# Mixture-of-experts tail: expert tiles of 128 slots in pairs, and second weights held in SBUF

## The reference, cut to what matters

```
logits = einsum('btd,ed->bte', x, w_router); probs = softmax(logits)
vals, idx = top_k(probs, 2); gates = sum(one_hot(idx, 8) * vals[..., None], -2)
acc = gelu(x @ Ws1.T + bs1) @ Ws2.T + bs2              # shared expert, 128 -> 512 -> 128
h = gelu(einsum('btd,efd->btef', x, W1) + b1)           # 8 experts, 128 -> 512 -> 128
y = einsum('btef,edf->bted', h, W2) + b2
out = SCALE * (acc + einsum('bted,bte->btd', y, gates))
```

## Time and profile before

| | |
|---|---|
| median of 3 runs (lowest to highest) | 633.46 us (633.27 to 637.78) |
| profiled execution | 635.85 us |
| its span, first to last instruction | 634.1 us |
| mean granted TensorE clock | 0.976 |
| TensorE matmul busy over the span | 576.8 us, 91% |

### The profile page before, as it was taken

The page is one execution under the profiler, slowest core; times in us unless marked ns, Lnnn a source line. Parts: engine busy times, 40 slices in busy tenths (PEclk is TensorE's granted clock), DMA queues, the critical chain, the costliest instruction groups (busy, mean ns, idle before and its releaser), DMA issues. The chain is left out here.

```text
span 634.1 us, 14457 instructions
## 1 busy us (share of the span) xinstructions
PE 576.8 (91%) x4324; PEld 512.9 (81%) x4324; DVE 427.3 (67%) x1730; ACT 333.7 (53%) x1064; POOL 389.8 (61%) x598
## 2 busy tenths in 40 slices
PE   2469999999999999999996967899999999999976
PEld 2249999899999999999984566788999999999952
DVE  3736888788788888878885579876553455545426
ACT  2455666566666656666662374894444444444410
POOL 1526666656666665666662607888888888887520
PEclk9999999999999999999998869899999999999989
DMA  9069930000000000000000001163564778777357
GB/s 196 6 260 394 395 150 1 2 0 0 0 0 0 0 0 0 0 0 0 2 2 1 2 0 39 45 231 95 156 186 130 216 244 247 230 235 232 103 201 212
DMA packets 39797, 66.77 MB, mean 105 GB/s; under 512 B 7523, under 2 KB 26725, under 8 KB 39749
## 3 DMA queue, kind: packets, MB, share of 16 engines
q1 hardware_dynamic: 31076, 54.85, 27.5%
q0 software_dynamic: 4544, 9.45, 4.2%
q10 hardware_dynamic: 4128, 1.91, 1.4%
HBM read 36.26 MB, written 29.92 MB: 104 GB/s over the span
## 5 line engine op out<-in xcount | busy, mean ns | idle before, releaser
L1575 ACT ACTIVATE hid<-bank,slab 128x256 f32<-128x256 f32 x156 | 64.2, 471 | 80.6 <-PE bank L1428 80.5
L1987 POOL DMA_INDIRECT ys<-yo,dst x78 | 75.2, 964 | 28.9 <-issue 16.6
L1979 POOL DMA_INDIRECT xs<-hrow,slot_i x64 | 62.7, 979 | 35.4 <-issue 35.4
L1442 PEld LDWEIGHTS bank<-slab,hid 128*128 128x128 f32 x624 | 75.8, 192 | 2.0
L1442 PE MATMUL bank<-slab,hid 128*128 128x128 f32 x624 | 76.0, 275 | 0.0
L1428 PE MATMUL bank<-hg,slab 128*128 128x256 f32 x312 | 73.7, 380 | 0.4 <-DVE hg L1842 0.4
L1875 DVE TENSOR_TENSOR yb<-bank,slab 128x256 f32<-128x256 f32 x39 | 16.6, 425 | 74.1 <-PE bank L1442 74.1
L1428 PEld LDWEIGHTS bank<-hg,slab 128*128 128x128 f32 x312 | 56.3, 190 | 6.7 <-issue 0.6
L986 POOL TENSOR_TENSOR nL<-aL,ones 128x128 f32<-128x128 bf16 x32 | 16.9, 528 | 41.4 <-ACT aL L695 41.4
L409 PE MATMUL bank<-aH,W2p 128*128 128x128 f32 x192 | 42.1, 301 | 0.1
L409 PE MATMUL bank<-kv,W1b 128*128 128x128 f32 x192 | 41.4, 298 | 0.0
(11 more groups left out here) (340 smaller groups left out, 1872.3 us busy)
## 6 DMA issues: line engine op xcount, KB each, us to landing
slab<-in_slabs_dram SPq DMA_DIRECT2D x39, 578.0 KB, 4.2
xs<-fill SPq DMA_DIRECT2D x34, 528.0 KB
xt<-xs SPq DMA_DIRECT2D x39, 132.0 KB
yg<-ys SPq DMA_DIRECT2D x8, 512.0 KB, 6.7
xr<-in_L_attn_x_dram SPq DMA_DIRECT2D x16, 128.0 KB, 6.9
ys<-yo,dst POOLq DMA_INDIRECT x78, 3.8
xs<-hrow,slot_i POOLq DMA_INDIRECT x64, 2.5
out_dram<-xr SPq DMA_DIRECT2D x16, 64.0 KB, 1.8
```

The lines of the kernel that those rows point to most:

```text
L1442: mm = pe.matmul(y[:, s * D:(s + 1) * D], hid[i % 2][:, n, s * P:(s + 1) * P], right, start=(n == 0), stop=(n == FT - 1), skip_group_check ...
L1575: nc.scalar.activation(hid[i % 2][:, n, :], e_half(i, n), ACT.Gelu_apprx_tanh, bias=bias).then_inc(e_x, 1)
L1979: pool.indirect_dma_start(out=xs[:, :], out_offset=bass.IndirectOffsetOnAxis(ap=slot_i[:, i, c:c + 1], axis=0), in_=hrow[:, c, :], in_offs ...
L1987: pool.indirect_dma_start(out=ys[:, :], out_offset=bass.IndirectOffsetOnAxis(ap=dst[v][:, s:s + 1], axis=0), in_=yo[v][:, s, :], in_offset ...
```

## The change

Tiles are allotted in halves of 128 slots, and a job is two halves that may belong to two different experts. 8192/128 + 7 = 71 halves, rounded up to 72, make 36 jobs in place of 39. `N_FULL` becomes 12. The list has 43 jobs; five shared ones still come before the second part of the expert jobs, now in front of expert job 12. The second weights of all 8 experts (2 MB) are loaded into SBUF once, at the start of the block, and TensorE addresses them by a register that it loads itself, two loads a job. The slab shrinks from 1156 to 644 numbers and is loaded twice a job, as are the rows, each half with its own register load on SP. `RW` goes from 5 to 4. The first matmul is done by halves: eight matmuls of 128 columns in place of four of 256; the gelu also, eight instructions in place of four.

```diff
-SLAB = 2 * F + FT + D
-N_TILES = (2 * B * S) // TS + E - 1
+SLAB = F + FT + D
+HALF = P
+N_HALVES = -(-((2 * B * S) // HALF + E - 1) // SUB) * SUB
+N_TILES = N_HALVES // SUB
-N_FULL = -(-(B * S - E * (TS - 1)) // TS)
+N_FULL = -(-(B * S - E * (HALF - 1)) // HALF) // SUB
+FULL = N_FULL * SUB
-RW = 5
+RW = 4
...
+            w2 = psb("w2", [P, E, F])
-            hid = [psb(f"hid{i}", [P, FT, TS]) for i in range(2)]
+            hid = hs
...
                 def weights(j):
                     if j >= RW:
                         sp.wait_ge(e_yb, job["expert", j - RW] + 1)
-                    e = sp.value_load(e_i[0:1, j:j + 1], min_val=0, max_val=E - 1)
-                    sp.dma_start(slab[j % RW][:, :], slabs[:, bass.ds(e, 1), :].rearrange("p o w -> p (o w)")).then_inc(s_slab[j % RW], 16)
+                    for s in range(SUB):
+                        e = sp.value_load(e_i[0:1, SUB * j + s:SUB * j + s + 1], min_val=0, max_val=E - 1)
+                        sp.dma_start(slab[j % RW][:, s, :], slabs[:, bass.ds(e, 1), :].rearrange("p o w -> p (o w)")).then_inc(s_slab[j % RW], 16)
                 def rows(j):
...
-                    row = sp.value_load(row_i[0:1, j:j + 1], min_val=0, max_val=XS_ROWS - TS)
-                    sp.dma_start(xt[j % RX][:, :, :], xs[bass.ds(row, TS), :].rearrange("(s p) w -> p s w", p=P)).then_inc(s_xt[j % RX], 16)
-
+                    for s in range(SUB):
+                        row = sp.value_load(row_i[0:1, SUB * j + s:SUB * j + s + 1], min_val=0, max_val=XS_ROWS - HALF)
+                        sp.dma_start(xt[j % RX][:, s, :], xs[bass.ds(row, HALF), :]).then_inc(s_xt[j % RX], 16)
+
+                sp.dma_start(w2[:, :, :], e_w2).then_inc(s_w2, 16)
                 sp.wait_ge(table_ready, 2)
...
                     for n in range(FT):
-                        mm = pe.matmul(e_half(i, n), left[:, n * P:(n + 1) * P], right, start=True, stop=True)
+                        if kind == "expert":
+                            for s in range(SUB):
+                                mm = pe.matmul(e_half(i, n)[:, s * P:(s + 1) * P], slab[j % RW][:, s, n * P:(n + 1) * P],
+                                               hg[j % 2][:, s * P:(s + 1) * P], start=True, stop=True)
+                        else:
+                            mm = pe.matmul(e_half(i, n), left[:, n * P:(n + 1) * P], right, start=True, stop=True)
...
                 def e_down(i):
+                    if kind == "expert":
+                        if j == 0:
+                            pe.wait_ge(s_w2, 16)
+                            pe.wait_ge(table_ready, 2)
+                        if j == N_FULL:
+                            pe.wait_ge(table_ready, 4)
+                        expert = [pe.value_load(e_i[0:1, SUB * j + s:SUB * j + s + 1], min_val=0, max_val=E - 1) for s in range(SUB)]
...
-                            right = slab[j % RW][:, F + n * P:F + (n + 1) * P] if kind == "expert" else sw[:, 1, n, :]
+                            right = w2[:, bass.ds(expert[s], 1), n * P:(n + 1) * P].rearrange("p o w -> p (o w)") if kind == "expert" else sw[:, 1, n, :]
...
-                        nc.scalar.activation(hid[i % 2][:, n, :], e_half(i, n), ACT.Gelu_apprx_tanh, bias=bias).then_inc(e_x, 1)
+                        if kind == "expert":
+                            nc.scalar.activation(hid[i % 2][:, n, 0:P], e_half(i, n)[:, 0:P], ACT.Gelu_apprx_tanh,
+                                                 bias=slab[j % RW][:, 0, F + n:F + n + 1])
+                            nc.scalar.activation(hid[i % 2][:, n, P:TS], e_half(i, n)[:, P:TS], ACT.Gelu_apprx_tanh,
+                                                 bias=slab[j % RW][:, 1, F + n:F + n + 1]).then_inc(e_x, 1)
```

More of the change, by code:

```diff
@@ L128, in program @@
         at = 0
-        for name, width in (("iota", E), ("down", E), ("tri", E * E), ("step", CAP // TS), ("tile", N_TILES), ("tau", CH), ("dump", SUB * RY), ("b2row", D)):
+        for name, width in (("iota", E), ("down", E), ("tri", E * E), ("step", CAP // HALF), ("tile", N_HALVES), ("tau", CH), ("dump", SUB * RY), ("b2row", D)):
             cut[name] = tabs[:, at:at + width]
@@ L1210, in program @@
             base, cnt, need, last = (psb(n, [P, E]) for n in ("base", "cnt", "need", "last"))
-            over = psb("over", [P, E, CAP // TS])
+            over = psb("over", [P, E, CAP // HALF])
             tri = psb("tri", [P, E, E])
-            past = psb("past", [P, N_TILES, E])
+            past = psb("past", [P, N_HALVES, E])
             full, taken, weight = psb("full", [P, E]), psb("taken", [P, E + 1]), psb("weight", [P, E])
-            first, rowf = psb("first", [P, N_TILES]), psb("rowf", [P, N_TILES])
+            first, rowf = psb("first", [P, N_HALVES]), psb("rowf", [P, N_HALVES])
             hs = [psb(f"hs{i}", [P, FT, SH]) for i in range(2)]
@@ L1218, in program @@
             xt = [psb(f"xt{i}", [P, SUB, ROW]) for i in range(RX)]
-            slab = [psb(f"slab{i}", [P, SLAB]) for i in range(RW)]
+            slab = [psb(f"slab{i}", [P, SUB, SLAB]) for i in range(RW)]
+            w2 = psb("w2", [P, E, F])
             hg = [psb(f"hg{i}", [P, TS]) for i in range(2)]
-            hid = [psb(f"hid{i}", [P, FT, TS]) for i in range(2)]
+            hid = hs
             yb = [psb(f"yb{i}", [P, SUB, D]) for i in range(2)]
@@ L1244, in program @@
             s_yg = [sem(f"s_yg{i}") for i in range(NG)]
-            s_slab = [sem(f"s_slab{i}") for i in range(RW)]
+            s_slab, s_w2 = [sem(f"s_slab{i}") for i in range(RW)], sem("s_w2")
             meta_step, meta_ready = sem("meta_step"), sem("meta_ready")
@@ L1573, in e_gelu @@
                         act.wait_ge(e_u, 2 * i + n // 2 + 1)
-                        bias = slab[j % RW][:, 2 * F + n:2 * F + n + 1] if kind == "expert" else sb1[:, n:n + 1]
-                        nc.scalar.activation(hid[i % 2][:, n, :], e_half(i, n), ACT.Gelu_apprx_tanh, bias=bias).then_inc(e_x, 1)
+                        if kind == "expert":
[3 more added lines that the diff above has]
+                                                 bias=slab[j % RW][:, 1, F + n:F + n + 1]).then_inc(e_x, 1)
+                        else:
+                            nc.scalar.activation(hid[i % 2][:, n, :], e_half(i, n), ACT.Gelu_apprx_tanh, bias=sb1[:, n:n + 1]).then_inc(e_x, 1)
                 def to_exp():
@@ L1784, in steps_over @@
                                                   op0=ALU.mult, op1=ALU.add))
-                    then(dve.scalar_tensor_tensor(out=over[:, :, :], in0=cnt[:, :].unsqueeze(2).broadcast_to([P, E, CAP // TS]),
-                                                  scalar=-float(spare), in1=cut["step"].unsqueeze(1).broadcast_to([P, E, CAP // TS]),
+                    then(dve.scalar_tensor_tensor(out=over[:, :, :], in0=cnt[:, :].unsqueeze(2).broadcast_to([P, E, CAP // HALF]),
+                                                  scalar=-float(spare), in1=cut["step"].unsqueeze(1).broadcast_to([P, E, CAP // HALF]),
                                                   op0=ALU.add, op1=ALU.is_gt))
@@ L1821, in full_tiles @@
                     row_of(ts, full, 0)
-                    then(dve.tensor_scalar(last[:, :], last[:, :], float(N_FULL), None, ALU.min))
+                    then(dve.tensor_scalar(last[:, :], last[:, :], float(FULL), None, ALU.min))
                     then(dve.memset(taken[:, E:E + 1], 0.0))
@@ L1827, in other_tiles @@
                 def other_tiles():
-                    ts = slice(N_FULL, N_TILES)
+                    ts = slice(FULL, N_HALVES)
                     steps_over(0)
```

46 lines of the change are left out of this document (22 added, 24 removed).

## The result

| | before | after |
|---|---|---|
| median of the runs beside each other | 635.62 us (633.27 to 640.31, 4 runs) | 652.57 us (646.65 to 654.83, 4 runs) |
| ratio, 95% interval | | 1.0226 (1.0163 to 1.0289) |
| profiled execution, span | 635.85, 634.1 us | 651.17, 649.4 us |

The change makes the kernel slower. The forecast was 642.5, with slower at 0.69: the sign and the range hold, the median lies 10 us above the number. Later runs of the same changed kernel gave 650.09 (ratio 1.0224, 1.0163 to 1.0285).

The account below looks back on a forecast made before the run. TensorE's matmuls were taken to bound the kernel before, SP's issues afterwards: TensorE's 9.4 us gain turns into waits for rows, net +9.0 us, so 642.5 us was forecast, own range 638 to 648, widened to 633 to 656.

Parts of the forecast that it names:

- TensorE's terms: On TensorE, three expert jobs less give -11.2 us; `e_up` in 128-column halves adds +1.8 over 36 jobs.
- SP's pace: SP's queue: four register loads and four DMAs take 4.63 us a job, against 3.79 that TensorE needs.
- The wait at job 12: TensorE stands about 3.8 us for job 12's rows, since the slabs of 12 and 13 are issued ahead of them.
- rival B: SP bounds, but half-size issues are cheaper, 1.05 to 1.09 us each: +1 to +4.5, 634 to 638 us; chance 0.15.
- The end: The last expert `e_down` on TensorE ends at 613.3 us instead of 604.30: +9.0 us.
- `e_up(0)` at 439.4: Start of the jobs on TensorE: the second job's rows come some 0.2 us late, so `e_up(0)` starts at 439.4.
- What was costed at nothing: TensorE's register loads, ScalarE's eight gelus, VectorE's longer `meta` and tables, POOL and the 2 MB load add nothing to the path.
- The tail: Bias, gate, scatter, loads of the final sum and stores behind the last expert `e_down` keep the same length.

Follow-up runs that it names:

- dearer ones alone: Kernel before with only slab and rows loaded in two halves, each with its own SP register load, 39 jobs: 660.00 us, ratio 1.0347.
- the other two parts: Kernel before with second weights resident and two TensorE register loads a job, 637.58 us; separately, kernel before with `e_up` in 128-column matmuls, 640.33 us.
- both edits: Changed kernel without the range check on SP's register loads and with job 12's rows issued ahead of slabs 12 and 13: 631.47 us, again 630.46.
- without the check: Changed kernel with SP's register loads made without their range check: 633.91 us, ratio 0.9975 to the kernel before.
- the rows first: Changed kernel with the rows of job 12 issued ahead of the slabs of jobs 12 and 13: 645.37 us.
- `e_up` by halves: Kernel before with only the expert `e_up` in 16 matmuls of 128 columns for 8: 640.33 us, ratio 1.0034.
- both edits with short pauses: Version of both edits with POOL's pause, a write of zeros, cut from 1408 to 352 columns: 628.12 us, again 627.98.
- The kernel before with short pauses: Kernel before with only POOL's pauses, writes of zeros, cut from 1408 to 352 columns: 634.13 us, ratio 0.9952.
- after, again: The changed kernel run and profiled once more, unchanged: 650.09 us, ratio 1.0224.

## Why the prediction was right, and where its number was off

**The mechanism** was the forecast's: SP, with over a third of its time free before, can't issue four register loads and four DMAs in TensorE's 3.79 us. It is shown from three sides: cheaper issues in the changed kernel give back 16 us of the job stretch, dearer ones alone cost the kernel before 24, and the other two parts that could have stopped TensorE cost 0.0 and 1.9.

**TensorE's terms.** -11.2 + 1.8 were measured whole: 155.6 to 155.8 us with both edits, 155.65 by the sum, and +1.9 for 39 halved `e_up`.

**SP's pace.** 4.63 a job was forecast. The steady pairs have 4.52 and 4.65. From the rows of job 12 (first issue 501.69) to those of job 35 (604.73) SP made 88 issues, since the rows of 12, 13 and 14 follow each other with no slab between: 103.0/88 = 1.17 us each. In it stand one wait for a free slab and five short ones for TensorE (window 500 to 610: us in total, times, longest):

```profile
SPq L1293 <- DVE yb L1897: 1.9, 1, 1.9
SPq L1301 <- PE bank L1417: 1.0, 5, 0.2
```

Without them an issue takes 100.1/88 = 1.14, between the forecast's 1.16 and rival B's 1.09 and nearer to the forecast. The two row issues of a pair are 1.09 apart (1.42 - 0.33), which is B's figure, but two slabs up to 1.18 (1.51), and from pair to pair in the same view, with a change of function between, it is 1.10 to 1.23. `feed` of job 12 to `feed` of job 35 took 607.93 - 505.19 = 102.7; the steps had 101.9.

**The wait at job 12.** 3.8 forecast, 3.57 measured, and 3.4 to 3.6 less when the order was turned. What it also cost I left out: behind it the shared `e_up` took 2.73 and the `e_down` 2.81, where 1.89 and 1.95 are usual (1.7 us together), with a granted clock of 0.95 for 486 to 520, so part of it was run at 1.2 GHz. In the version without the check the array stood for 2.77 at the same place, and the two had their usual length behind it:

```profile
499.45 0.44 PE L1419 MATMUL bank<-ident,xt 128*128 128x128 f32 x2 [2.77 <-DMA xt<-xs]
499.73 1.89 PE L1441 MATMUL bank<-hT,sw 128*128 128x256 f32 x8
```

The length of the stand alone doesn't decide it: with the rows first, a stand of 2.66 at another place was followed by an `e_up` of 3.58 where 1.95 is usual, and the granted clock was 0.83 from 540 to 550:

```profile
539.91 0.45 PE L1414 MATMUL bank<-ident,xt 128*128 128x128 f32 x2 [2.66 <-DMA xt<-xs]
540.18 3.58 PE L1433 MATMUL bank<-hg,slab 128*128 128x128 f32 x16
```

**The end.** 173.9 us were forecast from job 0's `e_up` to the last expert `e_down`; it was 175.0 and 174.8. Up to `feed` of job 12 forecast and run agree (61.1 each); the missing microsecond is 0.8 from there to `feed` of job 35 and 0.2 behind it. The forecast had no wait for a free slab there, and SP has the one of 1.9. It lies between the issues of 515.56 and 519.66, soon after the dip of the clock, which put the jobs off by 1.7; that the dip made it is likely, not shown.

**Where the number failed.** Its step "`e_up(0)` at 439.4" held in one profile of the changed kernel (438.72) and not in the other (444.06). It took the start of one execution for that of all. In the table the start splits into 438.0 to 439.3 and 442.5 to 445.1, with one at 441.29 between them, and the split goes with TensorE's granted clock from 380 to 386 in every row: 0.99 and 1.00 for the early ones, 0.62 to 0.76 for the others, whatever the program. So the early ones ran that stretch at 2.4 GHz and the late ones partly at 1.2; VectorE's routing then came later and met other holds by POOL. Most of the difference arises behind it: from POOL's first indirect DMA of the dispatch (380.2 to 383.3 in all profiles) to the start of the jobs it is 56.5 to 58.0 us in the seven early ones and 61.7 to 61.8 in five late ones, among them both profiles of both edits. These five have the same three holds by a pause, in the changed kernel's first profile the 1.84, 1.95 and 1.55 shown above; no early one has more than one. (`e_up` by halves, which starts at 442.48, has two and 59.9 us.) The profile that starts at 441.29 is both edits with short pauses: it has none of the three and takes 59.2. So about 2.5 us of the late start are what the pauses hold, by one profile against two. That the clock is the cause is an inference from this order of events; no run set it. The three runs of the kernel before that the prediction had, 633.27 to 637.78, held a hint of it: a spread of 4.5 us that it didn't ask about. Of the 10.1 us between 642.5 and 652.57, the median of the kernel before moved by 2.2 (633.46 to 635.62), the start made up to 4.7 (444.06 for 439.4), the job stretch 1.1 and what lies behind it 0.5; the rest is which runs were drawn.

**What was costed at nothing** stayed there. In the groups of 520 to 600 us TensorE has 9.6 us of idle time, all of it before `feed` and released by rows, so ScalarE's eight gelus and VectorE's `meta` hold nothing up. The 2 MB load was issued at 350.46 and landed in 8.8 us, over 80 us ahead of its first use. The larger tables are within 0.4% of nothing.

**The tail** behind the last expert `e_down` was taken as equal and isn't quite. Its 32 matmuls of the final sum follow an idle time in which the array waits for the scatter, and last from 14.0 to 17.1 us by the clock they get. The kernel before with short pauses had

```profile
612.79 14.02 PE bank L1520 x32
```

at a granted clock of 1.00 and the version of both edits

```profile
610.47 17.07 PE bank L1537 x32
```

at 0.82. In between are 15.7 (before, after and without the check, at 0.89) and 16.35 (after, again, 0.86). The eight profiles of the changed program and its versions have 15.6 to 17.1, the six with 39 jobs 14.0 to 17.0. Whether the changed program gets the low clock here more often is open.

## What to carry to other kernels

Count the issuing queue as an engine: a transfer whose address comes from a register costs SP 1.15 us here, against 0.5 for a static one, whatever its size, so that halving the tiles doubles it; the range check alone is 0.3 of it. Before a change adds issues, set issues times spacing against the time of a job on the engine that bounds, and look whether the queue still has slack at the places where its order was written for the old ratio. And when a kernel's runs spread by more than the effect, compare a stretch between two fixed events in the profiles, and the medians of many runs, not two totals.

## What the runs showed of the hardware

- Two register loads a job (0.94 us with their checks) in the queue of a TensorE that is full for 100 us cost the array nothing: 165.08 us against 165.05.
- On SP the range check of a loaded number makes 0.32 of 1.15 us (0.83 without it), about twice the length of its own two instructions in the changed kernel:

```profile
L1293 SPq FUSED_REGOPS  x72: 147/147/159, 422.2 to 607.6; - x72
L1293 SPq SEQ_ASSERT  x72: 18/18/18, 422.4 to 607.8; - x72
```

- VectorE instructions of 0.2 us last up to 2 when an elementwise operation or a memset of POOL runs beside them, and in six of eight cases in the changed kernel's first profile end with it within 0.1 us.
- The same program started its jobs at 444.06 and at 438.72, along with the clock granted 60 us earlier (0.71 and 1.00).
- After a 3.57 us stand the array ran the next 5.5 us partly at 1.2 GHz; after one of 2.77 it did not, and after one of 2.66 in another version it did again.
